# First router stage of a two-MoE macaron block: filler products on TensorE in every token block, weight rounding moved behind the blocks, root corrections, counts and remainders reordered

## The reference, cut to what matters

```python
def moe(x):                                   # h: 4096 x 256
    h = layernorm(x)
    probs = softmax(h @ router_w.T)           # 8 experts
    vals, idx = top_k(probs, 2); vals = vals / vals.sum(-1)
    for e in range(8):
        gate, up = split(h @ gate_up_proj[e].T)      # 2 x 176
        out += combine[:, e] * (silu(gate) * up @ down_proj[e].T)
    return out
x = x + 0.5 * moe(x)                          # first mixture: the changed stage leads to it
x = x + attention(layernorm(x))
x = x + 0.5 * moe(x)
```

## Time and profile before

| | |
|---|---|
| median of 3 runs | 793.61 us |
| lowest, highest | 789.54, 793.93 us |
| profiled execution, its time | 796.36 us |
| profiled execution, its span | 794.6 us |
| PE, DVE, ACT, POOL busy | 87%, 66%, 62%, 42% of the span |
| mean granted TensorE clock | 0.961 |
| first expert tile turned on PE | 81.54 us after the span's start |

### The profile page before, as it was taken

How to read it: one execution, slowest core, us unless ns; L and a number is a source line. 1 busy time by engine, 2 the same in 40 slices (tenths; PEclk the granted TensorE clock), 3 DMA queues, 4 the chain that set the end, 5 groups by cost and what they waited for, 6 DMA issues and landing times. The chain is left out here.

```text
span 794.6 us, 19426 instructions
## 1 busy us (share of the span) xinstructions
PE 690.0 (87%) x5468; PEld 603.7 (76%) x5468; DVE 528.2 (66%) x1813; ACT 490.2 (62%) x1734; POOL 335.8 (42%) x361
## 2 busy tenths in 40 slices
PE   3999799999999799998988889989635999999944
PEld 3976699999975688877767777778424999999833
DVE  6578566666656587786767576857664777777643
ACT  4766566666653587767766657767522666666633
POOL 5100544444416444455555545252551444444500
PEclk9999999999999999999999999999956999999979
DMA  9930354444422110011111111010124444444279
GB/s 313 279 110 13 124 147 141 143 130 127 128 82 85 39 41 28 28 41 55 55 55 48 61 41 48 22 55 2 61 91 117 132 128 125 128 131 126 83 288 346
DMA packets 57863, 83.40 MB, mean 105 GB/s; under 512 B 9520, under 2 KB 43827, under 8 KB 57780
## 3 DMA queue, kind: packets, MB, share of 16 engines
q1 hardware_dynamic: 44772, 47.63, 19.0%
q0 software_dynamic: 13008, 34.69, 14.0%
HBM read 45.77 MB, written 37.44 MB: 105 GB/s over the span
## 5 line engine op out<-in xcount | busy, mean ns | idle before, releaser
L1539 PE MATMUL CC<-w_hi,turned_parts 128*128 x568 | 172.5, 345 | 0.3 <-DVE turned_parts L1161 0.2
L655 POOL DMA_INDIRECT shared<-h_rows,tok_i x71 | 67.3, 948 | 119.0 <-issue 58.7
L667 POOL DMA_INDIRECT y_rows<-shared,y_dest x71 | 69.9, 985 | 88.7 <-DVE y_dest L1173 74.9
L683 POOL TENSOR_TENSOR pr<-pr,prec 128x1024 f32<-128x1024 f32 x31 | 58.8, 1895 | 112.2 <-DVE prec L1353 110.9
L1539 PEld LDWEIGHTS CC<-w_hi,turned_parts 128*128 128x128 f32 x568 | 103.8, 190 | 1.0 <-issue 0.9
L1539 PE MATMUL CC<-w_lo,turned_parts 128*128 x284 | 91.8, 323 | 0.0
L729 ACT ACTIVATE shared<-CC 128x176 f32<-128x176 f32 x142 | 45.1, 317 | 75.1 <-PE CC L1539 72.6
L813 ACT ACTIVATE pr<-SS,nmax 128x128 f32<-128x128 f32 x256 | 90.4, 400 | 0.8 <-issue 0.8
L700 POOL DMA_INDIRECT h_regions<-h_store,dest x64 | 63.1, 987 | 47.3 <-DVE dest L1256 27.3
L1156 DVE TENSOR_TENSOR shared<-shared,CC 128x176 f32<-128x176 f32 x142 | 48.0, 338 | 51.6 <-ACT shared L729 30.0
L691 POOL DMA_INDIRECT yg<-y_rows,slot_i x64 | 62.6, 977 | 34.9 <-DMA y_rows<-shared 15.5
(11 more groups left out here) (318 smaller groups left out, 2055.4 us busy)
## 6 DMA issues: line engine op xcount, KB each, us to landing
shared<-h_regions SPq DMA_DIRECT2D x71, 129.0 KB
y_rows<-shared SPq DMA_DIRECT2D x71, 128.0 KB
w_lo<-y_rows SPq DMA_DIRECT2D x9, 512.0 KB, 8.4
x_sb<-in_x_dram SPq DMA_DIRECT2D x8, 512.0 KB, 8.3
out_dram<-x_sb SPq DMA_DIRECT2D x16, 256.0 KB, 5.7
w_hi<-y_rows SPq DMA_DIRECT2D x7, 512.0 KB, 11.9
w_lo<-in_gupT_dram SPq DMA_DIRECT2D x2, 1408.0 KB, 10.7
h_regions<-pad_rows SPq DMA_DIRECT2D x15, 129.0 KB
```

What stands on the lines that cost most here:

```text
L655: pool.indirect_dma_start(out=rows[:, s % RING, 0:D], out_offset=None, in_=h_dram[:, :], in_offset=bass.IndirectOffsetOnAxis(ap=tok_i[:, s ...
L667: pool.indirect_dma_start(out=y_dram[0:TOPK * TOKENS, :], out_offset=bass.IndirectOffsetOnAxis(ap=y_dest[:, s:s + 1], axis=0), in_=y_sb[:, ...
L683: pool.tensor_tensor(pr[:, q, :, :], pr[:, q, :, :], prec[:, q, :].unsqueeze(2).to_broadcast([P, NH, P]), ALU.mult).then_inc(t["norm"], 1)
L1539: i = pe.matmul(CC[:, 512 * (u % 2):512 * (u % 2) + GU], rows_part[:, u % 2, c * P:(c + 1) * P], weights, start=(n == 1), stop=(n == 3 * DC))
```

## The change

- PE gets a loop `busy_clock(n)`: n products of a 128x128 tile of zeros with itself, 512 columns each, bf16, into a bank of `CC` that nothing uses then. 28 of them stand ahead of the router loop (behind a DVE memset of the tile), and one stands in every `turn(t)`, behind the two transposes and ahead of the logits of the tile before.
- ACT's `weights(e)` leave the router loop. They stand behind it: 0 and 1 first, then `lows(e)` and `weights(e + 2)` in turn; the attention weights come after e = 2.
- `PE_LOW` goes from 7 to 6: DVE makes the remainders of two experts, and does so behind `tok_i` and `at_i` where it was ahead of both.
- POOL corrects the root of piece 2 ahead of its constants; DVE takes all statistics ahead of its own `constants()`.
- PE's `first_counts` comes right behind `first_ranks(3)`, where `low_parts(2)` stood between; the later low parts move up by one place.
- DVE's `first_places(3)` comes ahead of the second half of `first_lanes(2, ...)`.
- Waits on `projb` count one more.

```diff
-PROJB_AT = 5
+PROJB_AT = 6
-WEIGHTS_AFTER = {22: 0, 25: 1, 28: 2, 30: 3}
-PE_LOW = 7
+PE_LOW = 6
+        idle_bf = rank4[:, :, :, :].rearrange("p i k e -> p (i k e)").bitcast(BF16)
...
-            correct_roots(stats_of[0:2])
+            correct_roots(stats_of[0:3])
             other_constants()
-            correct_roots(stats_of[2:])
+            correct_roots(stats_of[3:])
...
-                    if t in WEIGHTS_AFTER:
-                        weights(WEIGHTS_AFTER[t])
...
-                for e in range(4):
+                weights(0)
+                weights(1)
+                for e in range(PE_LOW):
                     lows(e)
-                    weights(e + 4)
-                a.wait_ge(loaded, 16 * len(loads))
-                attention_weights()
-                for e in range(4, PE_LOW):
-                    lows(e)
+                    weights(e + 2)
+                    if e == 2:
+                        a.wait_ge(loaded, 16 * len(loads))
+                        attention_weights()
...
             def first_layer():
                 r = R[0]
-                for c in range(4):
+                v.memset(idle_bf[:, :], 0.0).then_inc(projb, 1)
+                for c in range(len(STATS)):
                     first_stats(c)
                 constants()
-                for c in range(4, len(STATS)):
-                    first_stats(c)
...
+                first_places(3)
                 first_lanes(2, GROUP // 2, GROUP)
-                first_places(3)
                 first_starts()
...
-                for e in range(PE_LOW, E):
-                    low_part(e)
                 v.wait_ge(first["table"], 1)
                 v.tensor_scalar(tok_i[:, :], ...).then_inc(first["tokens"], 1)
                 v.wait_ge(first["turned"], 1)
                 v.tensor_scalar(at_i[:, 0:TABLE_TILES], ...).then_inc(r["weights_at"], 1)
+                for e in range(PE_LOW, E):
+                    low_part(e)
...
+            def busy_clock(n):
+
+                for _ in range(n):
+                    pe.matmul(CC[:, 0:512], idle_bf[:, :], idle_bf[:, :].unsqueeze(1).to_broadcast([P, 4, P]),
+                              start=True, stop=True, skip_group_check=True)
...
                     i.then_inc(z["transposed"], 1)
+                    busy_clock(1)
...
+            pe.wait_ge(projb, 1)
+            busy_clock(28)
             pe.wait_ge(rw_in, 16)
             pe.wait_ge(made, 3)
             first_router()
             pe.wait_ge(first["copied"], TILES + 2)
             low_parts(0)
             low_parts(1)
             first_ranks(GROUPS - 1)
+            first_counts()
             low_parts(2)
-            first_counts()
-            low_parts(3)
             pe.wait_ge(loaded, 16 * len(loads))
             weights_vo()
-            low_parts(4)
+            low_parts(3)
             bias_vo()
             for g in range(GROUPS - 1):
                 first_table(g)
-            low_parts(5)
+            low_parts(4)
             first_table(GROUPS - 1)
             turn_experts()
-            low_parts(6)
+            low_parts(5)
```

## The result

| | before | after |
|---|---|---|
| median of 4 runs each | 792.25 us | 803.05 us |
| lowest, highest | 789.54, 793.93 | 798.16, 807.61 |
| profiled execution, its time and span | 796.36, 794.6 us | 804.02, 802.3 us |
| mean granted TensorE clock | 0.961 | 0.922 |
| first expert tile turned on PE | 81.54 us | 93.52 us |

The kernel after takes 1.0135 of the time of the kernel before (95% interval 1.0096 to 1.0175). The first expert tile comes 12.0 us later, the medians differ by 10.8.

A forecast was written before the change was run, and what follows sets the result against it. PE in the router loop, at TensorE's lower 1.2 GHz, was taken to set the first expert tile's start. `tok_i` +9.7 and +1.3 behind it sum to +11.0: 804.6 us against 793.6, own range 801 to 807, wider range 784 to 808.

The forecast's parts named there:

- The clock falls at 13 to 17 us and stays down: Router loop on PE: early gaps drop TensorE to 1.2 GHz, and it stays there through the loop; chance 0.53.
- The weakest step: Router loop on PE: one filler a turn doesn't raise a low clock, as logits still hold over 40% of the time.
- Filler 26 x 0.40 = 10.4: PE, turns 6 to 31: each filler costs 0.40 us, 10.4 us in all, between 8.8 and 11.2.
- Root and weights, -0.9: Router loop: POOL's earlier root of piece 2 gains 0.6 us, ACT's weights moved out of the loop gain 0.3.
- Ranks 2 +9.5: PE at the router loop's end: ranks of the third group come 9.5 us later, bounds 7.9 to 10.3.
- Ranks 3 +9.6: PE behind the loop: ranks 3 stay behind low parts 0 and 1, which shift with the loop, so 9.6 us later.
- Places ahead of the lanes, 3.9 from ranks to `ecnt`: DVE behind ranks 3: half the lanes now follow the places, so 3.23 us becomes 3.9, a cost of 0.7.
- Remainder off the path, -0.6: DVE ahead of `tok_i`: moving the 1.48 us remainder gains only some 0.6 us, bounds 0.4 and 1.4.
- `tok_i` +9.7: End of DVE's routing work: `tok_i` comes 9.7 us later, from +9.6 + 0.7 - 0.6.
- First product 8.7 behind `tok_i`: PE's first expert product comes 8.7 us behind `tok_i` where it was 6.1, a cost of 2.6 us.
- Of those 2.6 us I took 1.3 as the net price: First expert tiles: their gaps win back part of the later first product, leaving 1.3 us, bounds 0 to 2.6.
- The rival that holds the clock: Router loop: the clock stays up, ACT sets the pace, `tok_i` at 67.6, time 785.5 us, bounds 784 to 788; chance 0.29.

The follow-up runs named there:

- the repeat: The kernel after, unchanged, run once more as a control on another chip: 1.0112 of the kernel before.
- bridged start: The kernel after with 8, 7, 3 and 3 fillers in turns 1 to 4 instead of one each: 0.9917 of the kernel before.
- burst: The kernel after with 14 fillers in turn 10 instead of one: 1.0049 of the kernel before.
- the kernel that stops its fillers: The kernel after with 8, 7, 3 and 3 fillers in turns 1 to 4 and none from turn 6 on: 0.9980 of the kernel before.
- the kernels without filler: The kernel after without fillers in turns, 0.9992 of the kernel before; the same with seven PE remainders and DVE's one ahead of `tok_i`, 0.9972.
- combined kernel with the moved low part: Kernel after plus 8, 7, 3, 3 fillers in turns 1-4, 8 ahead of ranks 2, low part 1 behind counts, high part 7 earlier: 0.9941 of before.

## Why the prediction was right

It gave 804.6 us, 1.0139 of its 793.6; measured were 803.05 and a ratio of 1.0135. Step by step:

- **The clock falls at 13 to 17 us and stays down.** It fell at 14.7 (at 16.1 in the repeat), as the granted clock shows, and rose only at 65.9, with the low parts. The cause given, the first turns with their gaps, is shown by the bridged start. The weakest step, that one filler doesn't raise a low clock, held as well. But its reason was half of the truth: the text treated rising and holding as one question about the content of a turn, and they are two. One filler a turn holds a high clock (bridged start, burst) and the loop without doesn't hold it (23.5 us in the kernel that stops its fillers).
- **Filler 26 x 0.40 = 10.4.** It is paid in full, 0.43 each, 11.3 us with against without; no weight load hides below it. The upper of the two bounds was right.
- **Root and weights, -0.9:** -1.6, as ranks 2 are at 49.75 without the filler instead of 51.37. This term was too small by 0.7 and the filler's by 0.8 to 0.9, and they offset each other: that `tok_i` came out so close is in part luck.
- **Ranks 2 +9.5:** +10.2 (61.58 - 51.37), or +9.1 in the repeat. **Ranks 3 +9.6:** +9.5. **Places ahead of the lanes, 3.9 from ranks to `ecnt`:** 3.86. **Remainder off the path, -0.6:** from `ecnt` to `tok_i` 12.47 instead of 13.26, -0.8. **`tok_i` +9.7:** +9.4.
- **First product 8.7 behind `tok_i`:** 8.93. The chain given (low part 5, high part 7, remainder 7, attention constants) is in the rows. A second one beside it, the gather held up by DVE's first remainder, wasn't foreseen. With DVE's wait for high part 7 gone and both remainders beside the gather, 7.7 us were left.
- **Of those 2.6 us I took 1.3 as the net price.** With `tok_i` counted apart, 2.5 of them are left at the ninth tile (24.13 behind `tok_i` against 21.62), 1.7 in the repeat (23.36), and 2.4 between the kernels without filler (24.14 against 21.72). This term was too small by 0.4 to 1.2. Later tiles give little back, and the clock, which the kernel before kept through its first tiles, fell at 93.2 us for 6.9 us behind PE's wait of 4.20.
- **The sum.** Measured at the ninth tile it is +11.9 (110.48 - 98.61) for +11.0 forecast. The difference of the medians is 10.8, that of the two profiled spans 7.7. The offset lasts to the end of the first mixture: its last tile is turned at 237.54 instead of 225.30. The profiled execution got its 4 us back in attention, whose code is untouched: from the first to the last `SS<-shared` product it took 298.0 us there, 306.1 in the kernel before and 307.0 in the repeat. Why, no run shows; so that 804.6 and 803.05 agree within 1.6 us is closer than the runs, which lie between 798 and 808, can bear out.
- **The rival that holds the clock** had 785.5 and `tok_i` at 67.6. The bridged kernel is this case, at 0.9917 x 793.6 = 787.0 with `tok_i` at 69.65. It was priced well but for two things: its terms add up to 50.3 us behind choice 3 where it says 50.8, so to 67.1 for `tok_i`; and ranks 3: the text had them in time, and PE's wait for DVE let the clock fall at 43.4.

## What to carry to other kernels

One filler a turn paid here only where the clock was up when the steady turns began: look for the first gaps, even of a microsecond, between the warm-up and the steady part, and fill those. In a loop whose clock had already fallen, the same filler was a plain cost, at the price of the low level. Where a loop sits at the low clock without a gap, one burst and then one filler a turn may bring it up and keep it there, so test both. A wait of PE behind the loop can undo it: the clock fell again in waits of 2.5 and 3.8 us. And before work is moved off a path on DVE, see which POOL instruction will now run beside it.

## What the runs showed of the hardware

- The same turn (two transposes, one 512-column product, four small logit instructions) kept TensorE at 1.2 GHz for 47 us in the kernel after and at 2.4 GHz for 24 us in the bridged one. A burst of 14 products moved it from one to the other within one turn.
- PE with next to no gap fell from 2.4 to 1.2 GHz when only transposes and 8-column products were left (busy 6.70 of 7.00 us, fall at 23.5, the last filler at 17.83). Busy time in the profile doesn't tell by itself what the clock will do.
- Two executions of the same kernel had the fall 1.4 us apart (14.7 and 16.1 us), and the rise too (65.9 and 67.4).
- The turn itself took 0.83 us at full clock and 1.60 at half, the same instructions; with three fillers 1.26 at full clock.
- DVE's two-input subtraction of 1.47 us held up an indirect gather instruction of POOL that started beside it: 0.97 us without, 1.65 with one, 3.04 with two in a row, in these two cases ending 0.84 to 0.85 us behind the last subtraction. In the combined kernel with the moved low part, two in a row stood beside it as well and it took only 1.73, ending 0.91 us ahead of the end of the second; the reason is open.
